# Batch 1's convolution by diagonal matmuls, batch 0's diagonals group by group on two engines, D*u as transposes, and small statistics moved off VectorE

## The reference

```python
# per batch; L = 256 tokens, d_inner = 256 channels, 16 states, 4 taps, dt_rank 8
x1  = einsum('bld,ed->bel', ctx, in_proj_w)
u   = silu(causal_depthwise_conv(x1, conv_w) + conv_b)          # 4 taps per channel
dt_low, B, C = split(einsum('bdl,ed->bel', u, x_proj_w))
dt  = softplus(dt_proj(dt_low) + dt_proj_b)
h_t = h_{t-1} * exp(dt_t * A) + (dt_t * u_t) * B_t              # 16 states per channel
y_t = sum_n h_t[n] * C_t[n]  + D * u_t
x   = x + tanh(g_xattn) * (y * silu(layernorm(x)))
# feed-forward: quantise rows of layernorm(x) with 127/max|.|, multiply by w13 (704 + 704),
# gated = relu(a)^2 * b, rmsnorm * norm_w, quantise again, multiply by w2
x   = x + tanh(g_ffn) * ffn(layernorm(x))
```

## Time and profile before

| what | value |
|---|---|
| three timed runs, median | 171.71 us (171.32 to 172.77) |
| the profiled execution, its own time | 171.11 us |
| its span, first to last instruction | 169.3 us |
| outside the span | 1.8 us |
| granted TensorE clock, mean | 0.998 of full speed |
| PE, DVE, ACT, POOL busy | 160.9, 136.9, 134.9, 107.9 us |

### The profile page before, as it was taken

One profiled execution on the slowest core, in us unless ns is written; L12 is line 12 of the kernel. 1 busy time (PEld: TensorE's weight loads), 2 busy tenths in 40 slices (PEclk: granted clock), 3 DMA queues, 4 the chain that ended last, 5 costly groups with the idle time before them and its releaser, 6 DMA issues.

```text
span 169.3 us, 3127 instructions
## 1 busy us (share of the span) xinstructions
PE 160.9 (95%) x1050; PEld 127.9 (76%) x1050; DVE 136.9 (81%) x210; ACT 134.9 (80%) x327; POOL 107.9 (64%) x72
## 2 busy tenths in 40 slices
...
GB/s 111 347 373 402 269 199 11 136 286 333 0 220 118 92 165 380 302 58 128 6 176 314 251 135 0 225 25 0 4 2 2 0 0 33 2 31 62 4 62 62
DMA packets 21745, 22.54 MB, mean 133 GB/s; under 512 B 13337, under 2 KB 14818, under 8 KB 21602
## 3 DMA queue, kind: packets, MB, share of 16 engines
...
HBM read 19.09 MB, written 3.26 MB: 132 GB/s over the span
## 4 chain that ended last, share of the span: by engine, by line
PE 88%; DVE 6%; DMA 3%; issue 1%; SPq 1%; ACT 1%
PE m_ps L925 33%; PE w_ps L979 17%; PE y_ps L949 17%; PE w_ps L995 10%; DMA ctxT<-in_ctxT 3%; PE w_ps L891 2%; PE w_ps L875 2%; DVE xc L719 2%; PE w_ps L883 2%; PE w_ps L986 2%; PE y_ps L937 2%; DVE xstat L749 2%; DVE bd L741 1%; PE w_ps L958 1%; PE w_ps L905 1%
## 5 line engine op out<-in xcount | busy, mean ns | idle before, releaser
L398 POOL TENSOR_TENSOR hb<-hb,cs 128x1024 f32<-128x1024 f32 x31 | 72.9, 2371 | 11.4 <-DVE hb L778 11.1
L778 DVE TENSOR_TENSOR_SCAN hb<-dA,m_ps 128x1024 f32<-128x1024 f32 x32 | 72.2, 2274 | 4.0 <-PE m_ps L925 1.6
L590 ACT ACTIVATE dA<-dt,nega 128x255 f32<-128x255 f32 (+1 forms) x160 | 58.9, 453 | 4.8 <-DVE hb L778 4.8
L925 PE MATMUL m_ps<-bd,duT 128*128 128x256 f32 (+1 forms) x224 | 60.4, 413 | 0.8 <-issue 0.7
L925 PEld LDWEIGHTS m_ps<-bd,duT 128*128 128x128 f32 x224 | 40.7, 190 | 10.5 <-issue 5.8
L949 PE MATMUL y_ps<-identf,hb 128*128 128x128 f32 x256 | 31.2, 273 | 0.0
L949 PEld LDWEIGHTS y_ps<-identf,hb 128*128 128x128 f32 x256 | 28.9, 141 | 1.7 <-issue 0.5
L979 PE MATMUL w_ps<-wT,xqT 128*128 128x352 bf16 x64 | 20.3, 317 | 0.0
L979 PE MATMUL w_ps<-wres,xqT 128*128 128x352 bf16 x64 | 20.2, 316 | 0.0
L979 PE MATMUL w_ps<-wlo,xqT 128*128 128x352 bf16 x64 | 19.9, 310 | 0.0
L422 POOL TENSOR_TENSOR gw<-gg,normw 128x704 f32<-128x704 f32 x7 | 11.8, 1687 | 12.7 <-DVE gg L820 6.7
...
## 6 DMA issues: line engine op xcount, KB each, us to landing
...
```

The source lines that it names most:

```text
L398: E.tensor_tensor(h_g, h_g, cs[:, s0:s0 + sn, l0:l0 + ln], ALU.mult).then_inc(hc_end if (b, i, h) == OUT_END else hc_ok[h], 1)
L590: last = act_fn(dA_g[:, s, 1:ln], dt[:, b, h, l0 + 1:l0 + ln], ACT.Exp, scale=nega[:, h, s0 + s:s0 + s + 1])
L778: V.tensor_tensor_scan(hb[:, k % 3, h], decays, inputs, 0.0, ALU.mult, ALU.add).then_inc(scan_ok[h], 1)
L925: last = T.matmul(m_q[:, :, c * P - l0:(c + 1) * P - l0], duT[:, p, c, h * P:(h + 1) * P], bd[:, (s0 + sn // 2 * q) // GN, c, n0:n0 + sn / ...
```

## The change

Five edits go in together.

1. Batch 1's convolution moves from DVE to PE. `tap/1.0` only copies x1 to `xc`; a new step `convp` for each half runs four matmuls, one for each tap, each with a diagonal of that tap's weights (`dcw`, made by POOL) and the tokens shifted; the silu then adds the bias from PSUM. Most of the `warm` steps go.
2. Batch 0's diagonals: one `bT` copies B to SBUF, and `bd` is one step for each group. Group 0 is made by DVE, groups 1 to 3 by POOL.
3. D*u: ACT multiplies u by D (`ud`, two instructions a batch), and `skip` becomes transposes that accumulate. `diag` goes.
4. Small statistics leave DVE: `xmr` and `outscale` go to POOL as chains of linked instructions, the floor of the two maxima becomes one more column of the tile that is reduced (written by ACT), and the multiplications by 127 and `finv` go to ACT.
5. The orders in `PLAN` are written anew.

```diff
+                elif name == "convp":
+                    pe.wait_ge(dcw_ok, i + 1)
+                    pe.wait_ge(free["act"], emptied("inproj", b, 0))
+                    ps = claim(name, b, i)
+                    for s in range(TAPS):
+                        last = T.matmul(ps[:, s:L], dcw[:, i, TAPS - 1 - s], xc[:, p, i, 0:L - s],
+                                        start=(s == 0), stop=(s == TAPS - 1))
...
+                    if b in CONV_PE:
+                        act_fn(xc[:, p].rearrange("p h l -> p (h l)"), bank("inproj", b, i),
+                               ACT.Copy).then_inc(free["act"], 1)
+                        continue
...
+                elif name == "u" and b in CONV_PE:
+                    act.wait_ge(work_full, full("convp", b, i))
+                    act_fn(u[:, b, i], bank("convp", b, i)[:, 0:L], ACT.Silu,
+                           bias=sm[:, S_CB + i:S_CB + i + 1]).then_inc(free["act"], 1)
...
+            if name == "dcw":
+                eng.wait_ge(l_sm, 16)
+                eng.wait_ge(ident_ok, 3)
+                E.tensor_tensor(dcw[:, i], identf[:, :].unsqueeze(1).broadcast_to([P, TAPS, P]),
+                                sm[:, S_TAP + TAPS * i:S_TAP + TAPS * (i + 1)].unsqueeze(2).broadcast_to([P, TAPS, P]),
+                                ALU.mult).then_inc(dcw_ok, 1)
+            elif name == "bd":
+                eng.wait_ge(free["dve"], emptied("bT", b, 0))
+                for c in range(HALVES):
+                    E.tensor_tensor(bd[:, i, c], identf[:, :].unsqueeze(1).broadcast_to([P, GN, P]),
+                                    bT[:, c, GN * i:GN * (i + 1)].unsqueeze(2).broadcast_to([P, GN, P]),
+                                    ALU.mult).then_inc(bd_ok[i], 1)
+            elif name == "xmr":
+                eng.wait_ge(xrs_ok, 1)
+                eng.wait_ge(xmv_ok, 1)
+                link(E.tensor_scalar(xt1[:, :], xmv[:, :, 1], EPS, None, ALU.add))
+                link(E.tensor_tensor(xt2[:, :], xrs[:, :], xrs[:, :], ALU.mult))
+                link(E.tensor_tensor(xt2[:, :], xt2[:, :], xt1[:, :], ALU.mult))
+                link(E.tensor_scalar(xt2[:, :], xt2[:, :], -0.5, 1.5, ALU.mult, ALU.add))
+                link(E.tensor_tensor(xrs[:, :], xrs[:, :], xt2[:, :], ALU.mult))
+                link(E.tensor_scalar(xt1[:, :], xmv[:, :, 0], -1.0, None, ALU.mult))
+                E.tensor_tensor(xmr[:, :], xt1[:, :], xrs[:, :], ALU.mult).then_inc(xmr_ok, 1)
+            elif name == "outscale":
+                hs = slice(i, i + 1) if b == BATCH - 1 else slice(0, HALVES)
+                y, v, t = grs[:, b, hs], gv[:, b, hs], gos[:, b, hs]
+                eng.wait_ge(grs_ok, b + 1 + i)
+                for h in tiles(b, i):
+                    eng.wait_ge(gc_ok[h], b + 1)
+                if b == 0:
+                    eng.wait_ge(gates_ok, 1)
+                link(E.tensor_scalar(v, ssq[:, b, hs], 1.0 / HID, EPS, ALU.mult, ALU.add))
+                link(E.tensor_tensor(t, y, y, ALU.mult))
+                link(E.tensor_tensor(t, t, v, ALU.mult))
+
+                link(E.tensor_scalar(t, t, gates[:, 2:3], gates[:, 3:4], ALU.mult, ALU.add))
+                link(E.tensor_tensor(y, y, t, ALU.mult))
+                E.tensor_tensor(t, gam[:, b, hs], y, ALU.mult).then_inc(gos_ok, 1)
...
+                elif name == "ud":
+                    await_u(act, b, HALVES - 1)
+                    if b == 0:
+                        act.wait_ge(work_full, full("inproj", BATCH - 1, 0))
+                    else:
+                        act.wait_ge(ud_free, b)
+                    for h in range(HALVES):
+                        last = act_fn(ud[:, h], u[:, b, h], ACT.Copy, scale=sm[:, S_D + h:S_D + h + 1])
+                    last.then_inc(ud_ok, 1)
...
-                            T.matmul(y_ps[:, t, h * P:(h + 1) * P], u[:, b, h, t * P:(t + 1) * P], diag[:, h],
-                                     start=(t == 0 and h == 0), stop=False, skip_group_check=True)
+                            last = T.matmul(y_ps[:, t, h * P:(h + 1) * P], ud[:, h, t * P:(t + 1) * P], identf[:, :],
+                                            start=(t == 0 and h == 0), stop=False, is_transpose=True,
+                                            skip_group_check=True)
...
                 elif name == "quant1":
...
+                    link(act_fn(fs[:, b, ts], fr[:, b, ts], ACT.Copy, scale=127.0))
                     for t in tiles(b, i):
...
+                    for t in tiles(b, i):
+                        last = act_fn(finv[:, b, t:t + 1], fam[:, b, t:t + 1], ACT.Copy, scale=frs[:, b, t:t + 1])
+                    last.then_inc(finv_ok, 1)
...
+                    link(act_fn(gc[:, b, i:i + 1], gr[:, b, i:i + 1], ACT.Copy, scale=127.0))
...
                 elif name == "absmax":
                     dve.wait_ge(gw_ok[i], b + 1)
-                    at = mark(V.tensor_reduce(gam[:, b, i:i + 1], gw[:, i], AX.X, ALU.max, apply_absolute_value=True))
-                    gamx[b, i] = at
-                elif name == "scale2":
...
+                    dve.wait_ge(grs_ok, b + 1 + (i if b == BATCH - 1 else 0))
+                    link(V.tensor_reduce(gam[:, b, i:i + 1], gw[:, i], AX.X, ALU.max, apply_absolute_value=True))
+                    V.reciprocal(gr[:, b, i:i + 1], gam[:, b, i:i + 1]).then_inc(gc_ok[i], 1)
...
                 elif name == "final":
...
+                    dve.wait_ge(gos_ok, b + 1 + (i if b == BATCH - 1 else 0))
```

More of the change, by code:

```diff
@@ L91 @@
     "pe": """
[L92 to L101, removed]
@@ L102 @@
-        down/0.1 iqT/1.1 down/1.0 xqT/3.1 down/1.1 iqT/2.0 up/3.2 up/3.3 iqT/2.1 down/2.0 iqT/3.0 down/2.1 iqT/3.1
-        down/3.0 down/3.1
+        warm/0.1 inproj/0.0 inproj/0.1 inproj/1.0 convp/1.0 xdbl/0.0 convp/1.1 dtproj/0.0 dtproj/0.1 bT/0.0 warm/0.0
+        duT/0.0 xdbl/1.0 inproj/2.0 duT/0.1 mix0/0.0 mix1/0.0 inproj/3.0 mix0/0.1 mix1/0.1 skip/0.0 mix0/0.2 sum0/0.0
+        mix1/0.2 sum1/0.0 mix0/0.3 sum1/0.1 xdbl/2.0 dtproj/1.0 sum0/0.1 xdbl/3.0 dtproj/2.0 dtproj/3.0 sum0/0.2
+        duT/1.0 mix1/0.3 szT/0.0 sum1/0.2 mix0/1.0 sum0/0.3 mix1/1.0 mix0/1.1 szT/1.0 sum1/0.3 duT/2.0 mix1/1.1
@@ L109 @@
[L109 to L117, removed]
+        tab/0.0 tap/0.0 gates/0.0 tap/0.1 u/0.0 tap/1.0 u/0.1 u/1.0 u/1.1 tab/0.1 soft/0.0 soft/0.1 tab/0.2 nega/0.0
@@ L118 @@
+        square/3.0 relu/3.2 rs2/3.0 relu/3.3 quant2/2.1 square/3.1 quant2/3.0 rs2/3.1 iqT/2.1 iqT/3.0 quant2/3.1
+        iqT/3.1
     """,
     "dve": """
-        conv/0.0 conv/0.1 conv/1.0 lowc/0.0 xstat/0.0 du/0.0 du/0.1 bd/0.0 xmr/0.0 bd/0.1 scan1/0.0 lowc/1.0 scan0/0.0
-        scan1/0.1 scan0/0.1 conv/2.0 conv/3.0 lowc/2.0 scan0/0.2 lowc/3.0 scan1/0.2 scan0/0.3 scan1/0.3 scan0/1.0
-        scan1/1.0 scan0/1.1 yz/0.0 x1/0.0 scan1/1.1 scan0/1.2 scan1/1.2 scan0/1.3 fam/0.0 scan1/1.3 scan0/2.0
@@ L123 @@
[L123 to L127, removed]
@@ L130 @@
+        final/3.1
     """,
     "pool": """
[L132 to L135, removed]
@@ L160 @@
 OUT_END = (BATCH - 1, NG - 1, 1)
-PRODUCTS = ("w_res", "w_lo", "du", "mul0", "mul1", "out0", "out1", "gated")
+PRODUCTS = ("dcw", "bd", "xmr", "outscale", "w_res", "w_lo", "du", "mul0", "mul1", "out0", "out1", "gated")
+CONV_PE = (1,)
 FILLS = {
-    "inproj": [("conv", "dve")], "xdbl": [("lowc", "dve")], "dtproj": [("soft", "act")], "bT": [("bd", "dve")],
+    "inproj": [("conv", "dve")], "xdbl": [("lowc", "dve")], "dtproj": [("soft", "act")], "bT": [("bT", "dve")],
+    "convp": [("u", "act")],
     "duT": [("duT", "act")], "szT": [("szT", "act")], "xqT": [("xqT", "act")],
```

218 lines of the change are left out of this document (114 added, 104 removed).

## The result

The changed kernel took **174.54 us** (median of four, 173.96 to 174.82) against 172.17 for the kernel before (171.32 to 172.77): a ratio of 1.0137, 95% interval 1.008 to 1.0194. The prediction was 168.3 with a range up to 171.3, and a chance of 0.10 for slower. It was wrong, and on the wrong side.

A forecast was written before the change was run, and what follows sets the result against it. PE's own chain of steps from the first mix was taken as the bound. A gain of 3.5 less a 0.5 pause, 3.0 us off 171.11, gave 168.1; 168.3 was named for timed runs, range 165.9 to 171.3.

The forecast's parts named there:

- a half costs 1.72: Head, PE: each convp half is four matmuls, priced at 0.86 us per two matmuls of 256 columns, so 1.72 us.
- there is nothing to win from the clock: Whole kernel: granted clock read as 1.00 in both listed stretches, so no gain was expected from it.
- the walk of the head: Steps before the first mix, walked with earlier durations: mix0/0.0 starts at 17.9 us, against 19.05 before.
- rival 2: POOL's diagonals are slow, 2.4 us for 512 elements, bd/0.3 comes late: 173.7 us, chance 0.09.
- The pauses at skip/0.0 and xdbl/2.0: Batch 0, PE: skip/0.0 waits for ACT's ud/0.0 and xdbl/2.0 for ACT's u/2.0, 1.0 us each.
- The skips: PE's D*u steps: four transposes at 0.44 us replace four fp32 matmuls at 0.89; three skips give -1.35 us.
- rival 5: The skip's transposes don't overlap like those of sum, so their records count in full: 170.7 us, chance 0.02.
- the rule: SBUF: a DVE instruction with two SBUF inputs and a GpSimd instruction reading SBUF shut each other out; bd/0.0 doesn't lose.
- PE did not wait for DVE in the middle: Middle of the kernel: the about 16 us DVE gives up were given no gain, except covering ACT's delays.
- The tail pause of 0.5: Last tile: down/2.1 waits for ACT's iqT/2.1, now behind quant2/3.0 and rs2/3.1, about 0.5 us.
- PE without pause from 60 us to the last tile: Sign to look for in the profile: PE runs with no pause between 60 us and the last tile.
- Rival 1: ACT's extra 7 us don't fit; a third, 2.3 us, comes through: 170.5 us, chance 0.17.

The follow-up runs named there:

- again, clock up: The changed kernel run once more with no edit, for its trace: 171.04 us, span 169.1.
- the two chains: Fastest follow-up kernel (batch 1's convolution on VectorE, more fillers, gated/2.0 held back, two order changes), 168.86 us, against it with D*u by matmuls again, 170.06 us.
- the filled gaps: The changed kernel with 5 transposes without use between batch 0's and batch 1's inproj and 6 ahead of convp: 171.41 us, ratio 0.9985 to before.
- the convolution on VectorE: The changed kernel with batch 1's convolution back on VectorE, fillers 10 and 8 around xdbl/0.0, 8 behind bT: 170.03 us, ratio 0.988 to before.

## Why the prediction was wrong, point by point

| step | predicted | the change, first trace | again, clock up |
|---|---|---|---|
| first mix starts | 17.9 | 22.10 | 18.23 |
| mix0/1.2 ends | 57.1 | 61.49 | 57.67 |
| PE's chain ends | 163.6 | 170.11 | 166.43 |
| span | 166.3 | 172.8 | 169.1 |

* **The step that failed first** is "a half costs 1.72" for convp. The price came from four records at the higher level, at 20.87 us in the earlier trace rows, and I put it at 8 us, where PE may be on the lower one. With it went "there is nothing to win from the clock": I took 1.00 of two late stretches for the whole kernel, and called the removed transposes a place that convp could take. They were what brings the clock up where it has not risen by batch 1's inproj. And each half of convp is eight records, the first half in front of xdbl/0.0, where the old kernel had nothing that batch 0 waited for. Measured: 3.7 us, in eleven of the change's seventeen executions by their times (one more lies between); three of them have a trace, two slow and one fast. What decides in a given execution stays open.
* **With the clock up the walk of the head was good**: 18.23 for 17.9, and 57.67 for 57.1. Its parts were less so. A diagonal on GpSimd took 1.01 us (four in 4.04), not 1.28, which refutes rival 2; seven linked small ones took 1.98, as predicted. The pauses at skip/0.0 and xdbl/2.0 exist but idle rows beside them are 0.2 and 0.5 us, not 1.0 each; the sums and dtproj around 40 us went at 1.02 to 1.06 instead of 0.87, which made up for it.

```profile
23.40 4.04 POOL L411 TENSOR_TENSOR bd<-identf,bT 128x512 f32<-128x512 f32 x4
...
30.69 0.66 PE L999 MATMUL y_ps<-identf,ctx 128*128 128x128 f32 x4 [0.19 <-ACT ctx L641]
...
39.69 1.06 PE L949 MATMUL w_ps<-u,xpwT 128*80 128x256 f32 x4 [0.53 <-ACT u L633]
```

* **The skips** cost 0.44 in the chain, as predicted, and rival 5 falls. In the whole kernel they gave 1.2 of 1.8: some of PE's gain is paid back. In the two chains the difference is 0.74 us at 112 us, where three skips with 1.35 lie behind, and 1.0 at the end, so most of the loss arises in the first three batches; ScalarE's 3 us of ud is the suspect, not shown.
* **Missed: out1/3.3 beside a GpSimd product.** I cited the rule, tried it on bd/0.0, where it costs nothing, and didn't try it on the three other VectorE products with two SBUF operands. The new order put gated/2.0 beside the one on which PE waits. 1.4 us, 1.6 by medians. It hangs on 0.2 us of order: it struck in the traces of the change and of the filled gaps and not in that of the convolution on VectorE.
* **Small statistics.** "PE did not wait for DVE in the middle" held: PE has no idle of note between 45 and 125 us. The tail pause of 0.5 is there (about 0.6: 25.5 us of PE steps lie in the 26.1 from sum1/3.3 to the end). Of the busy times ACT came out at 141.0 for 142 and POOL at 122.9 for 126; DVE was 124.8 for 120, so it gave up 12 us instead of 16, of which the long product is 1.4. "PE without pause from 60 us to the last tile" failed at 144 us alone, by those 1.4 us.
* **The sum.** 6.5 us separate the predicted span from the measured one. 3.7 is the clock, 1.4 the long product. Of the other 1.4, 0.6 arose before 58 us; the rest is spread over short holds like the two half-ups near 130 us, and their cause is not tested.
* **The rivals.** None was the right one. (Rival 1's 170.5 is 170.4 by its own terms, which changes nothing.) The clock was in none of them: I had seen the first fillers take longer than the later ones and made nothing of it.
